# A three-layer state-space network on one core: every third injection moved to GpSimd, its decay put over the B row in PSUM, a copy in three transfers, and four rotating slots

## The reference

```python
delta = jax.nn.softplus(delta + delta_bias[None, :, None])
def step(h, inp):
    dt, ut, bt, ct = inp
    dA = jnp.exp(dt[..., None] * A_k[None])
    dBu = dt[..., None] * bt[:, :, None, :] * ut[..., None]
    h = dA * h + dBu
    y = jnp.einsum('bkdn,bkn->bkd', h, ct)
    return (h, y)
```

## Time and profile before

| | us |
|---|---|
| median of 3 runs | 3905.7 (3900.73 to 3906.48) |
| the profiled execution | 3899.57 |
| its span, first to last instruction | 3897.8 |
| VectorE busy | 3266.7 (84%) |
| TensorE busy | 2856.5 (73%) |
| GpSimd busy | 2350.9 (60%) |
| ScalarE busy | 2051.6 (53%) |
| mean granted TensorE clock | 0.774 of full speed |

### The profile page before, as it was taken

How to read it: one execution, slowest core, us unless ns; L and a number is a source line. 1 busy time by engine, 2 the same in 40 slices (tenths; PEclk the granted TensorE clock), 3 DMA queues, 4 the chain that set the end, 5 groups by cost and what they waited for, 6 DMA issues and landing times. The chain is left out here.

```text
span 3897.8 us, 26756 instructions
## 1 busy us (share of the span) xinstructions
PE 2856.5 (73%) x6104; PEld 653.9 (17%) x6104; DVE 3266.7 (84%) x2104; ACT 2051.6 (53%) x2278; POOL 2350.9 (60%) x1004
## 2 busy tenths in 40 slices
PE   5768878887887788116576666778778877887887
PEld 2111111111111112011111112111111111111111
DVE  1899999999999995374888741999999999999993
ACT  3466565656555663113555424456564656656562
POOL 0677767777776764002565522677767867776773
PEclk9677788878788788557798778677787788778877
DMA  2655546564655553003424403564637555554642
GB/s 46 144 126 138 136 121 151 124 143 107 151 132 131 131 125 87 16 4 77 104 74 104 111 11 69 132 141 117 161 95 161 128 131 125 137 136 121 151 124 62
DMA packets 140331, 436.95 MB, mean 112 GB/s; under 512 B 33383, under 2 KB 34093, under 8 KB 139869
## 3 DMA queue, kind: packets, MB, share of 16 engines
q1 hardware_dynamic: 140188, 435.53, 46.4%
HBM read 307.50 MB, written 6.82 MB: 81 GB/s over the span
## 5 line engine op out<-in xcount | busy, mean ns | idle before, releaser
L809 POOL TENSOR_TENSOR L_read<-L_state,L_c_rows 128x1024 f32<-128x1024 f32 x768 | 1810.2, 2364 | 753.0 <-DVE L_state L900 470.9
L900 DVE TENSOR_TENSOR_SCAN L_state<-L_decay,L_b_ps 128x1024 f32<-128x1024 f32 x768 | 1755.8, 2286 | 29.0 <-DVE L_b_ps L885 1.9
L619 PE MATMUL L_y_ps<-L_read,L_fold 128*64 128x512 f32 x3072 | 1257.8, 914 | 394.3 <-POOL L_read L809 374.4
L885 DVE TENSOR_TENSOR L_b_ps<-L_du,L_b_ps 128x1024 f32<-128x1024 f32 x768 | 937.6, 1221 | 232.3 <-issue 143.5
L745 ACT ACTIVATE L_decay<-L_delta,L_a_neg 128x1024 f32<-128x1024 f32 x768 | 876.4, 1145 | 406.3 <-DVE L_state L900 405.4
L735 ACT COPY L_b_ps<-L_b_rows 128x1024 f32<-128x1024 f32 x256 | 260.0, 1016 | 340.6 <-DVE L_state L900 220.7
L619 PEld LDWEIGHTS L_y_ps<-L_read,L_fold 128*64 128x64 f32 x3072 | 188.5, 162 | 1355.1 <-POOL L_read L809 1013.1
L1417 POOL TENSOR_TENSOR L_read<-L_state,L_c_rows 128x1024 f32<-128x1024 f32 x96 | 236.7, 2471 | 201.3 <-PE L_y_ps L1213 113.4
L1525 DVE TENSOR_TENSOR_SCAN L_state<-L_decay,L_b_ps 128x1024 f32<-128x1024 f32 x96 | 219.5, 2286 | 3.3
L594 PE MATMUL L_side_ps<-L_dbl,L_w_dt 128*128 128x512 f32 x216 | 181.7, 937 | 49.5 <-DVE L_sq_b L871 26.9
L594 PE MATMUL L_side_ps<-g_cm,L_w_u 96*128 (+1 forms) x216 | 179.8, 921 | 44.9 <-ACT L_u L663 37.4
(11 more groups left out here) (313 smaller groups left out, 2760.7 us busy)
## 6 DMA issues: line engine op xcount, KB each, us to landing
L_c_rows<-L_bc_dram SPq DMA_DIRECT2D x580, 256.0 KB, 4.0
L_b_rows<-L_bc_dram SPq DMA_DIRECT2D x580, 256.0 KB, 4.2
L_delta<-L_delta SPq DMA_DIRECT2D x204, 256.0 KB, 5.8
L_du<-L_du SPq DMA_DIRECT2D x140, 256.0 KB, 5.7
L_du<-L_u SPq DMA_DIRECT2D x64, 256.0 KB, 6.0
L_bc_dram<-L_dbl SPq DMA_DIRECT2D x40, 128.0 KB, 3.4
L_delta<-L_delta_a SPq DMA_DIRECT2D x16, 256.0 KB, 5.9
L_du<-L_du_a SPq DMA_DIRECT2D x16, 256.0 KB, 6.5
```

Source lines behind the costliest of these rows:

```text
L619: m = nc.tensor.matmul(y_ps[i * BLK:(i + 1) * BLK, c, :], fold[:, :], y_half(t, o, i), start=first, stop=last, skip_group_check=True)
L809: nc.gpsimd.tensor_tensor(read[:, t % READS, :], state[:, t % STATES, :], c_rows[:, g % 2, :], ALU.mult).then_inc(multiplied, 1)
L885: nc.vector.tensor_tensor(to[:, :], du2[:, d * NBLK + c, :], row[:, :], ALU.mult).then_inc(injected, 1)
L900: nc.vector.tensor_tensor_scan(state[:, t % STATES, way], decay[:, t % DECAYS, way], fed[:, way], 0.0, ALU.mult, ALU.add).then_inc(scanned, 1)
```

## The change

1. **Motif copy.** The 127 partitions go in three DMAs, of 64, 48 and 15 partitions.
2. **Third injection.** In all scan layers the injection of a group's third tile is made by GpSimd, from du2 and `b_rows` in the state buffer into the state slot of that tile (`inject_c`). It stands ahead of the group's three reading products in GpSimd's order and waits for the reading product of the third tile of the group before, for the B rows and, in a turn's first group, for du2. VectorE scans that tile in place.
3. **Third decay.** ScalarE writes it over the B row in PSUM, once both of VectorE's injections of the group are done. Two decay buffers are left.
4. **B rows.** `b_rows` has two buffers with a semaphore each. A load waits for the copy and for GpSimd's injection two groups back.
5. **Conv layer slots.** delta2 and du2 have four slots for three blocks, and the slots rotate from image to image. The first block of the next image is copied behind the loads of its last group but one, the other two behind the last group's.

The tables of the side work and all other operations stay. The diff, cut to its core (the parts of the conv layer that repeat those of the cross-scan layers are left out):

```diff
-            sp.dma_start(below[0:127, :, :], f[1:128, :, :]).then_inc(below_ready, 16)
+            for a, z in ((0, 64), (64, 112), (112, 127)):
+                sp.dma_start(below[a:z, :, :], f[a + 1:z + 1, :, :]).then_inc(below_ready, 16)
...
-            dve.wait_ge(below_ready, 17)
+            dve.wait_ge(below_ready, 1 + 3 * 16)
...
-        decay = sb("decay", [128, DECAYS, L])
+        decay = sb("decay", [128, DECAYS - 1, L])
...
-        b_rows = sb("b_rows", [128, L])
+        b_rows = sb("b_rows", [128, 2, L])
...
                 sp.wait_ge(b_ready, G + 1)
+                sp.wait_ge(injected_c, G + 1)
                 for h in range(2):
                     row = p + NP * h
-                    sp.dma_start(b_rows[h * BLK:(h + 1) * BLK, :],
-                                 bc_dram[order, d, row:row + 1, :].to_broadcast([BLK, L])).then_inc(b_in, 16)
+                    sp.dma_start(b_rows[h * BLK:(h + 1) * BLK, g % 2, :],
+                                 bc_dram[order, d, row:row + 1, :].to_broadcast([BLK, L])).then_inc(b_in[g % 2], 16)
...
-            def copy_b(G, g):
-
-                act.wait_ge(b_in, 32 * (G + 1))
+            def copy_b(number, G, g):
+
+                act.wait_ge(b_in[g % 2], (number * (GROUPS // 2) + g // 2 + 1) * 32)
                 act.wait_ge(scanned, (G - 1) * NBLK + 2 + SCAN0)
-                nc.scalar.copy(b_ps[g % 2][:, :], b_rows[:, :]).then_inc(b_ready, 1)
+                nc.scalar.copy(b_ps[g % 2][:, :], b_rows[:, g % 2, :]).then_inc(b_ready, 1)
 
             def turn_of(turn):
                 o, number = turn.r, turn.number
                 for t, (d, p, c) in enumerate(tiles):
                     if c == 1:
-                        copy_b(number * GROUPS + p + NP * d, (p + NP * d))
+                        copy_b(number, number * GROUPS + p + NP * d, p + NP * d)
                     if p == 0:
                         act.wait_ge(delta2_in[d * NBLK + c], (number + 1) * PER_BLOCK)
                     act.wait_ge(scanned, number * NT + t - DECAYS + 1 + SCAN0)
-                    nc.scalar.activation(decay[:, t % DECAYS, :], delta2[:, d * NBLK + c, :], ACT.Exp,
+                    g = t // NBLK
+                    if c == 2:
+
+                        act.wait_ge(injected, (number * GROUPS + g) * 2 + 2 + INJECT0)
+                    to = b_ps[g % 2] if c == 2 else decay[:, c, :]
+                    nc.scalar.activation(to[:, :], delta2[:, d * NBLK + c, :], ACT.Exp,
...
+            def inject_c(number, g):
+
+                d, last = g // NP, NBLK - 1
+                if g % NP == 0:
+                    pool.wait_ge(du2_in[d * NBLK + last], (number + 1) * PER_BLOCK)
+                pool.wait_ge(b_in[g % 2], (number * (GROUPS // 2) + g // 2 + 1) * 32)
+                pool.wait_ge(multiplied, (number * GROUPS + g) * NBLK + MULT0)
+                nc.gpsimd.tensor_tensor(state[:, last, :], du2[:, d * NBLK + last, :], b_rows[:, g % 2, :],
+                                        ALU.mult).then_inc(injected_c, 1)
+
             def turn_of(turn):
                 number = turn.number
                 for t in range(NT):
                     g = t // NBLK
+                    if t % NBLK == 0:
+                        inject_c(number, g)
...
-                row = b_ps[g % 2]
                 if p == 0:
                     dve.wait_ge(du2_in[d * NBLK + c], (number + 1) * PER_BLOCK)
                 if c == 0:
-                    dve.wait_ge(b_ready, number * GROUPS + g + 2)
-                to = row if c == 2 else b_ps[1 - g % 2]
-                if c < 2:
-                    dve.wait_ge(scanned, T + SCAN0)
-                nc.vector.tensor_tensor(to[:, :], du2[:, d * NBLK + c, :], row[:, :], ALU.mult).then_inc(injected, 1)
+                    dve.wait_ge(b_ready, number * GROUPS + g + 1 + READY0)
+                to = b_ps[1 - g % 2]
+                dve.wait_ge(scanned, T + SCAN0)
+                nc.vector.tensor_tensor(to[:, :], du2[:, d * NBLK + c, :], b_ps[g % 2][:, :], ALU.mult).then_inc(injected, 1)
+                dve.wait_ge(injected, (number * GROUPS + g) * 2 + c + 1 + INJECT0)
                 return to
 
             def turn_of(turn):
                 number = turn.number
                 for t, (d, p, c) in enumerate(tiles):
-                    T = number * NT + t
+                    T, g = number * NT + t, t // NBLK
                     for at, key, i in turn.sides:
                         if at == t - DVE_LAG and key[0] in ("cent", "shift", "out"):
                             finish_side(turn, key, i)
-                    fed = inject_tile(number, t)
-                    dve.wait_ge(injected, T + 1 + INJECT0)
+                    if c < 2:
+                        by, fed = decay[:, c, :], inject_tile(number, t)
+                    else:
+                        by, fed = b_ps[g % 2], state[:, c, :]
+                        dve.wait_ge(injected_c, number * GROUPS + g + 1 + READY0)
                     dve.wait_ge(decay_ready, T + 1)
                     dve.wait_ge(multiplied, T - STATES + 1 + MULT0)
                     way = slice(None, None, 1 if d == 0 else -1)
-                    nc.vector.tensor_tensor_scan(state[:, t % STATES, way], decay[:, t % DECAYS, way],
...
+        def slot(image, q):
+            return (image * NBLK + q) % SLOTS
...
             def copy_block(image, q):
 
                 sp.wait_ge(sp_du, image * NJ + q // 2 + 1)
-                if image > 0:
-                    sp.wait_ge(decay_ready, (image - 1) * NT + NT - NBLK + q + 1)
-                copy_rows(delta2, delta, q, delta2_in[q])
-                if image > 0:
-                    sp.wait_ge(injected, (image - 1) * NT + NT - NBLK + q + 1 + INJECT0)
-                copy_rows(du2, du, q, du2_in[q])
+                was, last = divmod(image * NBLK + q - SLOTS, NBLK)
+                if was >= 0:
+                    sp.wait_ge(decay_ready, was * NT + NT - NBLK + last + 1)
+                copy_rows(delta2, delta, image, q, delta2_in[q])
+                if was >= 0 and last < 2:
+                    sp.wait_ge(injected, (was * NP + NP - 1) * 2 + last + 1 + INJECT0)
+                if was >= 0 and last == 2:
...
+                    if g == NP - 2 and turn.next is not None:
+                        copy_block(turn.next, 0)
                 if turn.next is not None:
-                    for q in range(NBLK):
+                    for q in range(1, NBLK):
                         copy_block(turn.next, q)
...
+            def inject_c(number, p):
+
+                G, last = number * NP + p, NBLK - 1
+                if p == 0:
+                    pool.wait_ge(du2_in[last], (number + 1) * per_block[last])
+                pool.wait_ge(b_in[G % 2], 32 * (G // 2 + 1))
+                pool.wait_ge(multiplied, G * NBLK + MULT0)
+                nc.gpsimd.tensor_tensor(state[:, last, :], du2[:, slot(number, last), :], b_rows[:, G % 2, :],
```

86 lines of the change are left out of this document (51 added, 35 removed).

## The result

The changed kernel takes 3956.05 us (median of 4 runs, 3949.04 to 3967.68), the kernel before, run beside it on the same chip, 3906.09 us (4 runs, 3900.73 to 3906.71). The ratio is 1.0134, with a 95% interval of 1.0103 to 1.0165: slower by 50 us. The prediction had 3812 us, between 3725 and 3900, and faster with a chance of 0.86. The profiled run of the changed kernel has a span of 3947.4 us against 3897.8.

The account below looks back on a forecast made before the run. VectorE was taken to bound the kernel, with a quarter of GpSimd's time free in cross scans. 3899.6 - 42.7 (motif) - 28 (cross) - 19 (conv) = 3810, plus 2 for the profiled run's place: 3812 us, range 3725 to 3900.

Parts of the forecast that it names:

- Motif copy: Motif layer: the copy split in three transfers is hidden and VectorE's idle wait goes, -42.7 us, bounds -42.7 and -25.
- The group lengths: Groups of three tiles: VectorE's falls from 10.62 to 9.45 us; GpSimd's, with a fourth product, takes 9.42 us.
- rival C: Third scan, an operand in SBUF written by GpSimd, collides like a tap: 0.94 us in 288 groups, about 4080; chance 0.03.
- ScalarE comes later: Third decay waits for both injections, delaying takes, side matmuls, y sums and GpSimd: 6 us a turn, bounds 0 and 12.
- First turns of later images: Cross layers, six turns: ten VectorE-bound groups 97.9 + 3, six GpSimd-bound 73.0 + 6; 179.9 us, -1.2 each, -7.
- Second turns: Cross layers, eight turns: GpSimd's 164.9 us of work, with waits 170.9 against 172.0; -1.1 each, -9.
- First turns of a layer: Cross layers, two turns: ten groups 94.5, six 70.7, waits 6; 171.2 us against 177.31, -6 each, -12.
- Conv layer: 32 VectorE injections fewer, -37 us; taps +10, late takes +8, slots 0; together -19, bounds -37 and 0.
- The late takes: Conv layer: ScalarE's late takes hold GpSimd there too, +8 us (0 to 23).
- B: Each late take exposes its full 3.2 to 5.0 us, GpSimd waits 14 us a turn: cross +100, 3938 us; chance 0.10.
- Rival A: GpSimd's own queue hides nearly all waits, turns near their floor: cross -120, conv -27, about 3710 us; chance 0.27.
- D: The motif copy is split but still slow, and 43 us stay: 3855 us; chance 0.05.

Follow-up runs that it names:

- the run without the gate: Changed kernel with the third tile's decay in a third SBUF buffer, so ScalarE waits for no injection: 4222.6 us, ratio 1.0831.
- the gate: Kernel before, with ScalarE's third-tile decay also waiting for VectorE's first two injections of the group, no work moved: 4073.8 us, ratio 1.0443.
- the motif run: Kernel before with the motif copy in three transfers and nothing else: 3857.9 us, ratio 0.9896.
- the slots run: Kernel before with the motif copy in three transfers and four rotating conv-layer slots, VectorE's injection as before: 3845.3 us, ratio 0.9852.
- with the order turned: Changed kernel with ScalarE's side work and next group's first decay ahead of the third decay: 3874.6 us; with fewer wait values to compute, 3864.3 us.
- with GpSimd's work lightened: Changed kernel with GpSimd's reading product of each third tile over half the columns: 3881.9 us, ratio 0.9954.
- the last choices of groups: Motif split, conv slots, GpSimd's injection in chosen cross-layer groups only, counts by tiles: narrower choice 3796.7 us; order fitted by group 3778.4 us.
- the first choice: Kernel before with motif split, conv slots, second B row, and GpSimd's injection only in chosen cross-layer groups (104 of 256): 3802.5 us, ratio 0.9744.
- the control: Same program as the first choice with no group chosen, so no GpSimd injection: 3880.9 us, ratio 0.9945.
- the same kernel with shared counts: The control again, no group chosen, with semaphore counts by tiles: 3850.2 us, ratio 0.9875.

## Why the prediction was wrong, point by point

**Motif copy: right.** -42.7 forecast, -42.5 measured alone.

**The group lengths: right.** Where VectorE doesn't wait, a group takes 9.46 us in the changed kernel (from the third scan at 3149.21 to that at 3158.67; 9.45 forecast), and GpSimd's four products take 9.33 us in a row (3146.79 to 3156.12; 9.31 before). The new third scan, with one operand in SBUF, takes 2.27 us: rival C was rightly put aside, and the run without the gate shows that its 0.94 us a group would have been too little for two operands in SBUF.

**ScalarE comes later: the step that failed.** The part saw the mechanism: the decay waits for both injections, and the takes queue behind it. It then followed one chain only, take, side matmul, y sum, reading product, and charged it to GpSimd with 6 us a turn. The other thing behind that decay in ScalarE's program, the copy of the B row that VectorE's next injection needs, was not followed: it has no term in the sum, and nothing says why. It is 250.9 us in the cross layers, 181.5 more than before, or 11.3 us a turn over 16 turns, and 61.2 us in the conv layer. The term that was charged was too small as well: in the second turn shown GpSimd idles 176.20 - 165.26 = 10.9 us, 9.2 of them for y sums, where 6 were forecast, while VectorE waits 16.7 us for copies and 8.1 for GpSimd's injection. But GpSimd's sum of work and waits is not what sets the turn, since 134 us less of its work shortened L3 by 26.8 only, and the gate cost 173 us where GpSimd had no work added. The right question was what stands behind the gate on ScalarE and who waits for each of those, copy included; the copy's due time is the end of the third scan, two scans (4.5 us) after the gate opens, and by the rows shown the gated decay, two takes, two softplus steps, the next decay and the copy take 6.2 us, with 2.4 more in which ScalarE waits for side matmuls.

**First turns of later images.** Ten groups were put at 97.9 + 3 and took 110.0; the last six at 79.0 and took 75.7. The 3 us were for ScalarE's six copies of y, the one place where work behind a decay was counted; the same holds for every take there. The last six were given 6 us of waits and had less. **Second turns:** 170.9 forecast, 176.2 measured; GpSimd was busy for 94% of it, not over 95%, but its idle time was put down to y sums and the third decay's to L903 (L885 before), as foreseen. **First turns of a layer:** 171.2 forecast, 172.7 measured, the closest; ten of their groups have hardly any side work, which fits but was not tried by itself. The cross sum was -28 and came out +48.5.

**Conv layer.** -19 forecast, +31 measured, outside the bounds of -37 and 0. The taps were right: all 36 took 71.8 us instead of 64.4, 7 more with 10 forecast. The late takes were sized at 8 (0 to 23) from GpSimd alone; VectorE's wait for copies grew from 14.4 to 61.2 us, 46.8, and it waits 16.3 us for GpSimd's injection and 25 more for side matmuls. With the injections' -37, the taps and 22 us less of waits for du this makes some 37, near the 31 measured. The slots, forecast at 0, were worth 12.6 by themselves. Beside GpSimd's injection they did what the forecast said, one wait for another: VectorE's 22 us less for du stand against 29.9 that GpSimd's injection waits for the third block's.

**The rivals.** B had the right mechanism's first half and came nearest, 3938 against 3956, for 0.10. The nearness of its number is partly luck: it had +100 in the cross layers where +48.5 came, and -19 in the conv layer where +31 came. It priced the delay on GpSimd, and its "against", that the free lag covers a part of each late take, is about GpSimd's lag, not about the copy. Rival A (3710) had GpSimd's queue hiding everything; GpSimd's queue can't hide a wait on VectorE. D is out by the motif run.

**The range and the chances.** The high end, 3900, was the forecast with twice its waits on GpSimd. No bound had been set for VectorE's waits for copies, although the prediction itself says of ScalarE's waits for B rows that VectorE stands behind them. B and C, both slower, have 0.13 together, while "slower" was given 0.10.

**What stays open.** How the 111 us between the slots run and the changed kernel split between gate and throughput: with the order turned, 19 us of them stay (3864.3 against 3845.3), with GpSimd's work lightened, 37 (3881.9 against 3845.3), and both at once wasn't tried. A third cost is in them that neither theory had. The changed kernel has 384 more register instructions on VectorE than the kernel before, and idles 37.7 us before 512 scans where it was 29.0 before 768, 18 us more than at the old rate. No run takes these alone out of it; the last choices of groups are without them.

## What to carry to other kernels

When an edit makes an in-order engine wait for something later, list everything that stands behind that instruction until the engine is idle again, and for each the one who waits and by when. The cheapest-looking item, here a copy of 1 us once in three tiles, can be the one that is due first. A change that pays in some groups and costs in others can be applied group by group: 98 of the cross layers' 256 places gave 67 us (3845.3 to 3778.4), all of them, with the conv layer's 32, cost 111. And measure a choice beside a control that has all of its bookkeeping: the first choice looked worth 43 us, and was worth 78 beside its own control.

## What the runs showed of the hardware that was not expected

- A scan on VectorE with both inputs in SBUF, beside GpSimd's products on SBUF, takes 4.15 us on the mean (median 4.23) instead of 2.27 to 2.29 with one input in PSUM; GpSimd's products beside it take up to 4.39 instead of 2.36. Beside the taps a product had lost 0.94 us, a good deal less.
- Register instructions for wait values of a loop aren't free for VectorE. In the control a scan started 0.21 us after its injection instead of 0.03, and 588 more such instructions came to 30.7 us of 3881 (against the same kernel with shared counts). With the order turned, where VectorE has other waits, 204 more of them cost 10 us.
- One wait, put into the kernel before with no work moved, cost 173 us, while VectorE's busy time in L3 stayed the same (1348.35 us against 1347.63).
